# Vision-transformer block on one core: a unit's token projection moved two turns ahead, its norm and query/key work three steps sooner

## What is computed

```python
h = einsum('bnd,de->bne', patches16x16(x), W) + b          # 64 x 196 tokens, 768 -> 192
h = h + attn(layernorm(h))      # 12 heads of 16; rotary q, k; causal; weights erf(scores) + 1, over their sum
h = h + ffn(layernorm(h))       # 8 experts, top 2, capacity; plus a shared expert (width 768)
```

## Time and profile before

| | |
|---|---|
| median of 3 runs | 4115.49 us (4110.92 to 4119.64) |
| profiled execution, its own time | 4127.77 us |
| its span, first to last instruction | 4126.0 us |
| busy in the span | PE 3536.0, weight loads 2519.4, VectorE 2485.9, ScalarE 1703.6, GpSimd 1411.1 us |
| granted clock of PE, mean | 0.83 of 2.4 GHz |
| attention stage | from the start to about 1952 us |

### The profile page before, as it was taken

How to read it: one execution, slowest core, us unless ns; L and a number is a source line. 1 busy time by engine, 2 the same in 40 slices (tenths; PEclk the granted TensorE clock), 3 DMA queues, 4 the chain that set the end, 5 groups by cost and what they waited for, 6 DMA issues and landing times. The chain is left out here.

```text
span 4126.0 us, 80390 instructions
## 1 busy us (share of the span) xinstructions
PE 3536.0 (86%) x28468; PEld 2519.4 (61%) x28468; DVE 2485.9 (60%) x4827; ACT 1703.6 (41%) x3390; POOL 1411.1 (34%) x1302
## 2 busy tenths in 40 slices
PE   6999898899989989997221199999999999999998
PEld 5777676677767767775210056666666666666665
DVE  6887877787788778777630045555455444444543
ACT  3444544444444444443000034444444444444443
POOL 1222222222222222222247600003555555555555
PEclk8877777777777777776555599999999999999999
DMA  1111111110111111011010022222323323223222
GB/s 64 33 41 48 49 33 41 49 48 29 44 48 34 39 49 48 29 45 40 29 45 1 1 64 68 72 64 65 61 39 59 55 41 62 38 58 60 39 38 33
DMA packets 166694, 186.08 MB, mean 45 GB/s; under 512 B 45263, under 2 KB 145711, under 8 KB 162319
## 3 DMA queue, kind: packets, MB, share of 16 engines
q1 hardware_dynamic: 95696, 123.03, 9.2%
q0 software_dynamic: 57472, 48.46, 7.9%
q10 hardware_dynamic: 13262, 10.65, 0.7%
HBM read 107.75 MB, written 67.85 MB: 43 GB/s over the span
## 5 line engine op out<-in xcount | busy, mean ns | idle before, releaser
L1235 DVE SCALAR_TENSOR_TENSOR ffn_hidden<-ffn_up,ffn_silu 128x490 f32<-128x490 f32 (+2 forms) x534 | 358.1, 672 | 1018.9 <-ACT ffn_silu L1218 777.1
L656 POOL TENSOR_TENSOR weights<-weights,x_pair 128x400 f32<-128x400 f32 x384 | 395.0, 1029 | 1227.4 <-DVE weights L521 720.3
L1218 ACT ACTIVATE ffn_silu<-ffn_gate 128x490 f32<-128x490 f32 (+2 forms) x534 | 310.9, 582 | 919.1 <-PE ffn_up L1186 673.9
L1204 PE MATMUL ffn_out<-ffn_w_lo,ffn_hidden_hi 128*126 128x192 f16 (+2 forms) x2124 | 523.9, 247 | 20.9 <-issue 20.9
L1203 PE MATMUL ffn_out<-ffn_w_hi,ffn_hidden_hi 128*126 128x192 f16 (+2 forms) x2124 | 524.2, 247 | 20.0 <-issue 20.0
L1205 PE MATMUL ffn_out<-ffn_w_hi,ffn_hidden_lo 128*126 128x192 f16 (+2 forms) x2124 | 524.0, 247 | 19.3 <-issue 19.3
L570 DVE RECIPROCAL recip<-x_product 128x200 f32<-128x200 f32 x384 | 535.4, 1394 | 0.0
L1377 POOL DMA_INDIRECT tokens<-dram_x,ids x256 | 280.5, 1096 | 738.9 <-issue 601.9
L1387 POOL DMA_INDIRECT out_rows<-done,kept x256 | 419.4, 1638 | 158.5 <-issue 95.4
L740 PE MATMUL bank<-w_tok,patches 128*128 128x192 f32 x1536 | 365.7, 401 | 13.9 <-DVE ident L486 13.9
L1182 PE MATMUL ffn_gate<-ffn_tokens_near_hi,ffn_w_hi 128*128 128x490 f16 (+2 forms) x534 | 201.2, 377 | 197.3 <-issue 113.6
(11 more groups left out here) (185 smaller groups left out, 8014.0 us busy)
## 6 DMA issues: line engine op xcount, KB each, us to landing
patches<-in_patches SPq DMA_DIRECT2D x32, 1176.0 KB, 5.2
ffn_raw<-in_w SPq DMA_DIRECT2D x18, 768.0 KB
dram_x_t<-x_t SPq DMA_DIRECT2D x32, 392.0 KB, 2.5
x_t<-dram_x_t SPq DMA_DIRECT2D x24, 512.0 KB
base<-dram_h SPq DMA_DIRECT2D x24, 384.0 KB
out_rows<-sums ACTq DMA_DIRECT2D x24, 384.0 KB, 4.7
v_held<-v SPq DMA_DIRECT2D x64, 102.0 KB, 2.4
dram_h<-h SPq DMA_DIRECT2D x32, 192.0 KB
```

Of the source, the lines that this page charges most:

```text
L656: nc.gpsimd.tensor_tensor(weights[:, n % 4], weights[:, n % 4], x_pair[:, n % 4, ::-1], ALU.mult)\
L1204: nc.tensor.matmul(out, hi, w_lo[:, m, :], start=False, stop=False)
L1218: nc.scalar.activation(T.silu[:, m % 2, 0:n], T.gate[m % 2][:, 0:n], ACT.Silu, scale=1.0 / (TOKEN_SCALE * WEIGHT_SCALE)).then_inc(T.silued, 1)
L1235: nc.vector.scalar_tensor_tensor(T.hidden[:, m % 2, 0:n], T.up[m % 2][:, 0:n], HIDDEN_SCALE / (TOKEN_SCALE * WEIGHT_SCALE), T.silu[:, m % ...
```

## The change

The table of positions has a new order, and with it each engine's turn. The token projection leaves steps 0 to 3 of the turn before its unit's pairs; it runs at the end of the turn before that, two tiles each in steps 10 and 11, so in turn u for unit u + 2. PE's blocks of a "mid" turn now stand so: step 3 transposes of the normed tokens and half the query/key/value product, step 4 the other half and y's transposes, step 5 output projection, step 8 transposes of x2 and three query/key transposes, step 9 routing and the other three, step 11 the next unit's first scores, steps 10 and 11 tokens. On VectorE bias and statistics stand at step 0, the norm at step 1, rotation at steps 3 and 4, low parts at 5 and 6, ahead of h2's addition and x2's norm, which stay. A turn "pre" with the first unit's tokens comes in front, a turn "late" without tokens near the end, and the loop has 14 trips, with one "mid" turn behind it. The load of patches runs two units ahead, and SP's stores of h2 and x2 come behind its copy of v. The diff, cut to its core:

```diff
-TOK, YT, PROJ, LN1T, QK, VV, X2T, ROUTE, QKT = (
-    (0, 1), (2, 3), (4, 5), (6, 7), (8, 9, 11, 12), (10, 13), (14, 15), (16,), tuple(range(17, 23)))
-NEXT = TOK + LN1T + QK + VV + QKT
+LN1T, QK, VV, YT, PROJ, X2T, QKT, ROUTE, TOK = (
+    (0, 1), (2, 3, 5, 6), (4, 7), (8, 9), (10, 11), (12, 13), (14, 15, 16, 18, 19, 20), (17,), (21, 22))
+NEXT = LN1T + QK + VV + QKT
 PREV = YT + PROJ + X2T + ROUTE
 TURNS = {
-    "pro": NEXT,
-    "first": NEXT,
-    "mid": NEXT + PREV,
+    "pre": TOK,
+    "pro": NEXT + TOK,
+    "first": NEXT + TOK,
+    "mid": NEXT + PREV + TOK,
+    "late": NEXT + PREV,
     "last": PREV,
     "end": PREV,
 }
+MIDS = UNITS - 3
...
+    turn("pre", -2, 0, 0)
     turn("pro", -1, 0, 1)
     turn("first", 0, 0, 0)
-    with eng.Fori(0, (UNITS - 2) // 2) as j:
+    with eng.Fori(0, (MIDS - 1) // 2) as j:
         turn("mid", 2 * j + 1, j, 1)
         turn("mid", 2 * j + 2, j, 0)
+    closing_turns(turn)
...
+    turn("mid", UNITS - 3, (UNITS - 4) // 2, 1)
+    turn("late", UNITS - 2, (UNITS - 3) // 2, 0)
     turn("last", UNITS - 1, (UNITS - 2) // 2, 1)
     turn("end", UNITS, (UNITS - 1) // 2, 0)
```

SP:

```diff
-            sp.dma_start(patches[0][:, 0:KP * UT], dram["patches"][0:128, :]).then_inc(patches_in[0], 16)
+            for s in range(2):
+                sp.dma_start(patches[s][:, 0:KP * UT], dram["patches"][s * 128:(s + 1) * 128, :]).then_inc(patches_in[s], 16)
...
-                    if kind == "mid":
-
-                        sp.wait_ge(normed_ready, 4 * u)
-                    sp.dma_start(patches[prev][:, 0:KP * UT], dram["patches"][bass.ds((u + 1) * 128, 128), :])\
+                    sp.wait_ge(normed_ready, 4 * u + 8)
+                    sp.sem_inc(x2t_spacer, 1)
+                    sp.dma_start(patches[prev][:, 0:KP * UT], dram["patches"][bass.ds((u + 3) * 128, 128), :])\
                       .then_inc(patches_in[prev], 16)
```

ScalarE (the bodies that only change their step are left out):

```diff
                 for n in range(PAIRS):
+                    if pairs and n < PAIRS - 1:
+                        copy_scores(u, n + 1, kind == "first" and n < 3)
+                    if n == PAIRS - 1 and has_next:
+                        copy_scores(u + 1, 0, kind == "pro")
...
-                    if n in (1, 3) and has_next:
-                        if kind != "pro" and n == 1:
-
-                            act.wait_ge(h_kept, u + 1)
-                        copy_out(TOK[n // 2], h_new[:, n - 1:n + 1, :].rearrange("p t d -> p (t d)"), 128, 2 * D)
+                    if n == 3 and has_next:
+                        for k, pos in enumerate(LN1T):
+                            copy_out(pos, normed_t[:, k * UT:(k + 1) * UT], KD)
+                    if n in (3, 4) and has_next:
...
-                    if n in (8, 9) and has_next:
-                        for t in range(2 * n - 16, 2 * n - 14):
+                    if n in (5, 6) and has_next:
+                        for t in range(2 * n - 10, 2 * n - 8):
 
                             act.wait_ge(qk_rotated, 4 * u + 5 + t)
...
-                    if n == 11 and has_next:
-                        for g in range(6):
+                    if n == 8 and has_next:
+                        for g in range(3):
+                            copy_out_qk(g)
+                    if n == 9 and has_next:
+                        for g in range(3, 6):
                             copy_out_qk(g)
+                    if n in (10, 11) and has_tokens:
+                        if kind != "pre" and n == 10:
+
+                            act.wait_ge(h_kept, u + 2)
+                        copy_out(TOK[n - 10], h_new[:, 2 * n - 20:2 * n - 18, :].rearrange("p t d -> p (t d)"), 128, 2 * D)
```

VectorE:

```diff
-                    if n == 3 and has_next:
-                        out_of(TOK)
+                    if n == 0 and has_next:
+                        dve.wait_ge(free[TOK[-1] % NB], tokens_filled(kind, u))
                         nc.vector.tensor_tensor(h_new[:], h_new[:], over(bias[:], [128, 4, D]), ALU.add)\
                           .then_inc(biased, 1)
                         dve.wait_ge(biased, u + 2)
                         spread_of(0, h_new)
-                    if n == 4 and has_next:
+                    if n == 1 and has_next:
                         norm(0, root_number(kind, u, 0), h_new, normed, normed_ready)
...
-                    if n in (6, 7) and has_next:
+                    if n in (3, 4) and has_next:
...
-                    if n in (8, 9) and has_next:
-
-                        for t in range(2 * n - 16, 2 * n - 14):
+                    if n in (5, 6) and has_next:
+
+                        for t in range(2 * n - 10, 2 * n - 8):
                             dve.wait_ge(qk_hi, 8 * u + 8 + 2 * t + 2)
...
+                    if n == 5 and has_prev:
+                        out_of(PROJ)
+                        dve.wait_ge(h_kept, u)
+                        step(nc.vector.tensor_tensor(h2[prev][:], h2[prev][:], h[prev][:], ALU.add))
+                        spread_of(1, h2[prev])
+                    if n == 6 and has_prev:
+                        norm(1, root_number(kind, u, 1), h2[prev], x2[prev], x2_ready)
```

PE:

```diff
+                    if n == PAIRS - 1 and has_next:
+                        copied(QKT)
+                        scores("first" if kind == "pro" else "mid", u + 1, 0, qk_t[prev])
...
-                    if n < 4 and has_next:
-
-                        if n == 0:
-                            pe.wait_ge(patches_in[prev], 16 * (prior + 2) if kind == "mid" else 16)
...
+                    if n == 3 and has_next:
+                        pe.wait_ge(normed_ready, 4 * u + 8)
+                        transposed(LN1T, normed)
+                        copied(LN1T)
+                    if n in (3, 4) and has_next:
+                        for t in range(2 * n - 6, 2 * n - 4):
+                            out = room(QK[t])
+                            product(out[:, 0:2 * D], normed_t, t, qkv_w, 2 * D).then_inc(full[QK[t] % NB], 1)
...
-                    if n == 9 and has_prev:
+                    if n == 8 and has_prev:
                         pe.wait_ge(x2_ready, 4 * u)
...
+                    if n == 8 and has_next:
+                        pe.wait_ge(roped, 4 * u + 8)
+                        for g in range(3):
+                            transpose_qk(g)
+                    if n == 9 and has_prev:
                         copied(X2T)
                         out = room(ROUTE[0])[0:E, 0:UT]
...
-                    if n == 11 and has_next:
-                        pe.wait_ge(roped, 4 * u + 8)
-                        for g in range(6):
+                    if n == 9 and has_next:
+                        for g in range(3, 6):
                             transpose_qk(g)
...
+                    if n in (10, 11) and has_tokens:
...
+                        tokens(2 * n - 20)
+                        tokens(2 * n - 19)
```

More of the change, by code:

```diff
@@ L108 @@
 }
+KINDS = tuple(TURNS)
+MIDS = UNITS - 3
 NB = 2
@@ L633, in _ @@
                 turn("mid", 2 * j + 2, j, 0)
-            chain.leave((UNITS - 2) // 2)
-            turn("last", UNITS - 1, (UNITS - 2) // 2, 1)
-            turn("end", UNITS, (UNITS - 1) // 2, 0)
+            chain.leave((MIDS - 1) // 2)
+            closing_turns(turn)
         @block.gpsimd
@@ L720, in transpose_qk, with tokens @@
                     last.then_inc(full[pos % NB], 1)
-                for n in range(PAIRS):
-                    if pairs:
-                        if n < PAIRS - 1:
-                            scores(kind, u, n + 1, qk_t[slot])
-                        if n >= LAG:
-                            if n == LAG:
-                                pe.wait_ge(held_in[slot], 32 if kind == "first" else 32 * (prior + 1 - slot) + 32)
-                            attend(kind, u, n - LAG, v[slot], v_held[slot])
+                def tokens(n):
+                    pos, at = TOK[n // 2], n % 2 * D
+                    out = room(pos) if n % 2 == 0 else bank[pos % NB]
+                    for i in range(KP):
+                        last = nc.tensor.matmul(out[:, at:at + D], wide(patches[slot], i, n), tok_w[:, i, :],
+                                                start=(i == 0), stop=(i == KP - 1))
+                    if n % 2:
+                        last.then_inc(full[pos % NB], 1)
@@ new lines, in turn @@
+                for n in range(PAIRS):
+                    if pairs and n < PAIRS - 1:
+                        scores(kind, u, n + 1, qk_t[slot])
+                    if n == PAIRS - 1 and has_next:
+                        copied(QKT)
+                        scores("first" if kind == "pro" else "mid", u + 1, 0, qk_t[prev])
+                    if pairs and n >= LAG:
+                        if n == LAG:
+                            pe.wait_ge(held_in[slot], 32 if kind == "first" else 32 * (prior + 1 - slot) + 32)
+                        attend(kind, u, n - LAG, v[slot], v_held[slot])
@@ new lines, in turn @@
+                    if n in (3, 4) and has_next:
```

(8 more changed lines are left out.)

143 lines of the change are left out of this document (56 added, 87 removed).

## The result

The changed kernel takes 4352.3 us (median of 4 runs, 4345.74 to 4354.54), the kernel before 4117.57 in the same session (4 runs, 4110.92 to 4121.72): a ratio of 1.0537 with a 95% interval of [1.0502, 1.0571]; the two medians divided give 1.0570, at the upper end of it. By the medians it is 235 us slower; 4387 was forecast, with a range of 4270 to 4480.

A forecast was written before the change was run, and what follows sets the result against it. PE was taken to set the pace where its clock is low. Middle turns 1940, back edge 42, first turn 55, tokenless turn 55.8: 2093 against 1835, +258; prologue +13.6; +271 on 4115.5 gives 4387 us, range 4270 to 4480.

The forecast's parts named there:

- What bounds the kernel: In the 31 turns, PE sets the pace where its clock is low; VectorE waits some 12 us a turn.
- The two new waits: PE waits for the norm before step 3's transposes, about 3 us, and for x2 before its transposes, 5.6 us.
- VectorE's wait for the casts: Before its first low part VectorE waits for ScalarE's four casts, queued behind the output projection's copies: 2.3 us lost.
- the likeliest case: The layout itself, chance 0.64: two clock rises a turn, near product and tokens, mean near 0.70; turns near 67 us.
- The half product: Query/key/value product after the norm's wait, starting at the low clock: 6.93 us until the next scores, against 4.1 at full clock.
- The prologue: Opening before the turns: second unit's tokens 6.8 + 4.3, second load of patches 3.5, minus 0.99: +13.6 us.
- the back edge stays, 14 x 3.0 = 42: PE's idle time at the loop's jump, once in two turns, remains 3.0 us in each of 14 trips: 42 us.
- the middle turn itself: One middle turn laid out from step 0's scores at 66.9 us; 29 of them make 1940 us.
- A: Rival, faster: the clock outlives both waits and stays at 2.4 GHz all turn; turn 57.5 us, total 4098; chance 0.06.
- B: Rival, milder: clock stays up from tokens into step 3, falls after step 5; turn 63.4 us, total 4285; chance 0.13.
- C: Rival, worse: two tiles of tokens all at low clock, and part of the next; total 4462 us; chance 0.14.
- D: Rival, no effect: the new waits take only time PE would have idled; total 4115 us; chance 0.03.

## Why the prediction was right, and where its sum was off

**What bounds the kernel** held: VectorE's work in the stretch is unchanged, and the 205 us of its growth are 153 of PE's idle time and 52 of its slower instructions. The Trainium skill's page "Perfetto Trace Analysis", section "Identifying the Most-Contended Engine", would have the engine with the highest occupancy optimized first, here VectorE. The trace does not agree that this move fed it: its statistics and norm did move into its starved stretch, and it idled 18.4 us a turn afterwards instead of 12.

**The two new waits** were there as laid out: for the norm 2.9 us a turn (3.2 forecast), for x2 5.7 (5.6). VectorE's wait for the casts was 2.3 us (2.3), and taking it away shortened the wait for x2 by 2.3, so the chain behind it was right too. Routing's wait is gone.

**The clock** did what the likeliest case has: two rises a turn, in the product and in the tokens, mean 0.71 (0.70). The half product took 6.30 us up to the next scores (1000.70 to 1007.00), where 6.93 was taken from the first turn; the first two tiles 6.13 against 6.8; the second two 4.17 against 4.3.

**The prologue** came to +14.7 us (+13.6), the two loads of patches in front costing 3.0 (16.93 for 13.93; 3.5 taken). VectorE's idle time in a turn was 18.4 us (19).

**What was mis-sized**: by the spans the sum was +271 and came to +226.6, 45 us too much (by the medians +235, and 35 too much in the time). All of it is in the 31 turns: 2040.4 us, not 2093, which is 53 less; opening and later stages were 8 more than taken. The main term is "the back edge stays, 14 x 3.0 = 42". It shows 0.74 us here (the last row of PE's turn above; 9.0 us in the 13 edges between 100 and 1880 us), so 14 x 0.74 = 10, 32 less. The prediction took this term over from the earlier trace rows and did not ask what would stand ahead of the jump. The rest is the middle turn itself: consecutive loads of patches are issued 66.3 and 66.9 us apart (998.72, 1064.98, 1131.88), 66.6 on average with half an edge of 0.74 in it, so 66.2 without, against 66.9; 29 x 0.7 = 20. The tokens and the half product, 0.67 and 0.63 us shorter than taken, are more than enough for that.

**The rivals.** A (4098, the clock outlives both waits) fell with the rows at 0.50 above; its price was near the right one for what it named: with fillers in both waits the changed kernel has 0.9997 of the time of the kernel before, where A's 4098 is 0.9957, though the clock in the 1600 us was then 0.88 and not 1.00. B (clock up into step 3) fell with the product's 6.37 us, C (both tiles of tokens all at the low clock) with 6.13 instead of 8.4. D fell with the result.

**What stays open**: why the clock falls where it does, for PE had run light pairs for 4 us before the fall at 1022.3 without a wait; how the 235 us divide between the tokens' move and the sooner norm, or whether they can be divided at all; and whether another spread of the tiles avoids both low-clock starts of the kernel with two tiles at step 8 and two at step 11.

## What to carry to other kernels

Price a new wait on a throttled PE at its length plus what runs slower behind it: here a wait of 5.7 us cost about its own length and about 5 us more after it, and one of 2.9 us another 2.2 after it. Before moving a heavy block, look at what it leaves behind: a stretch of small products only is where this clock fell and where the next wait opened, and the best place found here for a movable block was ahead of the longest wait. Where no work is left for it, a counted number of constant products, no longer than the wait, won 65 to 155 us; a count twice as high won nothing.

## What the runs showed of the hardware that was not expected

The idle time at the loop's back edge depends on what stands ahead of the jump. With transposes, scores or light pairs just ahead of the jump it is 2.96, 2.92 and 3.67 us in the rows shown (the kernel before, tokens at steps 7 and 8, fillers in the kernel before), and 3.4, 2.6, 3.4 and 3.3 us on average between 100 and 1880 us in these three and in the kernel with one tile in each of steps 8 to 11. With 24 matmuls of the token projection just ahead of it, it is 0.74, on average 0.7. That long work in the queue hides the jump is argued from these placements; no run changed this alone. The Trainium skill's page "Runtime: NRT & Kernel Launch", section "Instruction fetch mechanics", says that a taken branch to a page that is not at hand has to fetch it before the engine goes on; no run here shows the fetch itself.

A clock of 0.93 instead of 0.75 over 1600 us of the attention stage bought only 1.7% of the whole time, and one of 0.91 instead of 0.70 in the changed kernel with 28 and 16 fillers bought nothing. The mean granted clock alone says little about the time; it has to be read beside what ran while it was high.
